# One store for an output that goes to four places, earlier query loads, and accumulations and weight loads spread out

## The chip, the cores and the metric

The kernel runs on one core of a Trainium2 chip. The time is what the device needs for one launch, in microseconds (us); three runs of the kernel before gave 1413.55, 1416.99 and 1418.76, median 1416.99. One further execution was taken with the hardware profiler; the page and the trace rows below are of that one. The engines are TensorE (PE in the rows; PEld is its weight load), VectorE (DVE), ScalarE (ACT), GpSimd (POOL) and SyncE (SP, whose DMA queue is SPq). They run their own instruction streams in order and wait for each other through semaphores.

## The reference

A pre-norm decoder layer in float32 on 2 batches of 512 rows of width 1024. The first block is causal attention with 32 query heads and 8 key/value heads of 128:

```python
q = (hidden_states @ Wq).reshape(B, S, nh, hd).transpose(0, 2, 1, 3)
k = (hidden_states @ Wk).reshape(B, S, nkv, hd).transpose(0, 2, 1, 3)
v = (hidden_states @ Wv).reshape(B, S, nkv, hd).transpose(0, 2, 1, 3)
q = _apply_rope(q, cos, sin)
k = _apply_rope(k, cos, sin)
logits = jnp.einsum('bhqd,bhkd->bhqk', q, k) * scale
attn = jax.nn.softmax(logits.astype(jnp.float32), axis=-1).astype(q.dtype)   # after the causal mask
out = jnp.einsum('bhqk,bhkd->bhqd', attn, v)
return out.transpose(0, 2, 1, 3).reshape(B, S, nh * hd) @ Wo
...
x = x + _L0_attn_ref(_layernorm(x, axis=-1), L0_attn_Wq, L0_attn_Wk, L0_attn_Wv, L0_attn_Wo)
x = x + _L0_xattn_ref(_layernorm(x, axis=-1), ctx_4096, ...)   # fake-quantised product, 1024x1024 per batch
x = x + _L0_ffn_ref(_layernorm(x, axis=-1), ...)               # low-rank experts, top 16 of 64
```

## The kernel before, in words

Every float32 product is made of three passes over a high and a low part (float32r), and the big products (queries, keys, values, output) use seven block products in place of eight. The seven are called P1 to P7.

From about 194 to 950 us of the span the program is a loop over 64 **units** `u`, one head of one batch each. `u // 8` is the key/value group, `u % 8 // 4` the batch. On TensorE a unit is: `scores(u)`, a place for work, `mix(u - 1)` (probabilities times values), a second place, `turn_probs(u)` (ten transposes of the probabilities); where a unit has a third place, it came between the second and `turn_probs(u)`. A **place** holds a **job**, one of the seven block products of a pair of query or key heads that a later unit will need. Units 3, 5, 8, 12 and 16 have three jobs, units 50 and 52 one, unit 56 none, the others two. From unit 57 on the places hold steps of the output projection (`first_step`).

For a job, ScalarE rounds a piece of the weight to its high part (`narrow_high`), GpSimd makes the low part (`narrow_low`), TensorE multiplies into one of two banks (`job_bank`, even and odd jobs), and VectorE reads the bank (`read_job`). So job j+2 waits until job j has been read. The results of jobs P4 and P3 are rotated: GpSimd ends the rotation (`turn_added`), and SyncE stores it to `qk_dram` (`keep_turned`), from where `load_q` fetches one head of one batch (256 KB) two units ahead. ScalarE needs that load in `q_high(u + 1)`, which stands right behind `probs_high(u - 1)` at the start of its unit u, ahead of the exponentials.

The output of a unit lies in bank 5 (`mixed`). ScalarE copies it to `o_st[u % 2]` (`keep_out`), and SyncE stores it. The output projection is also done with seven products, so it needs sums of quarters of the attention output: A00, A01, N11 (a negated A11), S1, S2, S3, S4. The stores put an output into every array of which it is the first summand: `O_STORES` names them, four arrays for the units 0 to 31 of batch 0 (16 units), one array for every other unit. The other summands are added in DRAM: GpSimd issues DMAs that accumulate 1 MB each (`accumulate`), three in a row at the end of its unit u when u % 8 is 2, and one when u % 8 is 6 from unit 32 on.

Then come 48 **steps** of the output projection (`step`, 24 matmuls each, from 950.5 us), six products of eight steps. A step needs 512 KB of `oraw` from DRAM (`load_step`) and a pair of rows of blocks of Wo, which lies in four buffers w00, w10, w11, w01 of eight pieces of 512 KB (`load_wo_early`: two pieces a unit from unit 53 on, 16 in all; the other 16 two a step in steps 2 to 9). After that the second and third blocks of the layer run, which the change does not touch.

The order on each engine is written out by hand in the loops over `u` (lines 605, 822, 1021, 1380 and 1617 in the profile's numbering).

## Time and profile before

| what | value |
|---|---|
| median of 3 runs | 1416.99 us |
| profiled execution | 1417.59 us |
| its span, first to last instruction | 1415.8 us |
| TensorE busy | 1297.9 us (92%) |
| VectorE, ScalarE, GpSimd busy | 830.5, 771.2, 611.3 us |
| mean granted TensorE clock | 0.966 of full |
| SyncE's DMA queue (q1) | 176.79 MB, 38.3% of the DMA engines' time |
| GpSimd's DMA queue (q0) | 29.36 MB, 10.5% |

TensorE is busy for 92% of the span. The page's idle column names for each group of instructions who released it; the forty slices show that TensorE's busy share falls below nine tenths at the start, in single slices of the unit loop, around 850 to 1000 us, and at the end.

### The profile page before, as it was taken

The page shows a single profiled execution, that of the slowest core. Times are in us where ns is not written, and L with a number is a line of the kernel's source. Part 1 is how long each engine was busy: PE and PEld are TensorE (multiplying, and loading weights), DVE is VectorE, ACT ScalarE, POOL GpSimd, SP SyncE. Part 2 cuts the span into 40 slices and gives each one's busy share as a digit, 9 for nine tenths or more (in the row PEclk, how much of TensorE's full clock was granted, in tenths as well). Part 3 has the DMA queues.
Part 4 walks back from the last instruction along what each step waited for, and adds up shares of the span by engine and source line. Part 5 has one row for each costly group of instructions (what it writes and reads, how often), then busy time and mean ns, then how long its engine had stood idle before and what let it go on. Part 6 is the DMA issues. An engine that isn't in the chain of part 4 may idle for free. (4 is left out here: it accounts for less than half of the span.)

```text
span 1415.8 us, 19913 instructions
## 1 busy us (share of the span) xinstructions
PE 1297.9 (92%) x7025; PEld 1111.4 (78%) x7025; DVE 830.5 (59%) x1805; ACT 771.2 (54%) x1587; POOL 611.3 (43%) x454
## 2 busy tenths in 40 slices
PE   4999998999799998999999978797999998987998
PEld 4879997778678887888888867685888887766777
DVE  7687134354455554555656555353786778787863
ACT  4412246565566775777777767672333355465440
POOL 5676656566477665777776644220000000021000
PEclk9899999999899999999999998898999999999999
DMA  7033144437638548467385756849643385200001
GB/s 252 8 127 120 62 146 159 122 102 181 205 97 206 196 141 254 142 152 196 104 223 146 185 159 214 241 132 290 250 137 117 123 270 188 91 1 16 31 30 45
DMA packets 117122, 207.42 MB, mean 147 GB/s; under 512 B 10128, under 2 KB 51088, under 8 KB 113440
## 3 DMA queue, kind: packets, MB, share of 16 engines
q1 hardware_dynamic: 112992, 176.79, 38.3%
q0 software_dynamic: 4032, 29.36, 10.5%
q8 instruction: 56, 0.92, 0.3%
q14 instruction: 42, 0.34, 0.1%
HBM read 147.40 MB, written 88.08 MB: 166 GB/s over the span
## 5 line engine op out<-in xcount | busy, mean ns | idle before, releaser
L1215 DVE TENSOR_TENSOR pT_lo<-banks,pT_hi 128x512 fp32r<-128x512 f32 (+1 forms) x192 | 104.0, 596 | 234.2 <-ACT pT_hi L953 234.0
L1790 POOL TENSOR_TENSOR resid<-resid,colterm 128x1024 f32<-128x1024 f32 x8 | 19.9, 2493 | 370.8 <-ACT colterm L1847 281.2
L1553 PE MATMUL banks<-xc,nring_hi_b 128*128 128x512 f32 x448 | 148.1, 413 | 20.0 <-DVE n_u L1165 8.0
L1595 PE MATMUL banks<-ob_hi,oa_hi 128*128 128x512 f32 x384 | 152.1, 396 | 12.7 <-DVE ob_lo L1247 12.7
L1595 PE MATMUL banks<-ob_lo,oa_hi 128*128 128x512 f32 x384 | 151.5, 394 | 0.0
L1595 PE MATMUL banks<-ob_hi,oa_lo 128*128 128x512 f32 x384 | 151.1, 393 | 0.0
L1553 PE MATMUL banks<-xc,nring_hi_a 128*128 128x512 f32 x448 | 140.9, 396 | 5.9 <-DVE q_made L1165 5.9
L953 ACT CAST pT_hi<-banks 128x512 fp32r<-128x512 f32 (+1 forms) x192 | 86.8, 523 | 107.3 <-PE banks L1523 107.1
L937 ACT CAST oa_hi<-oraw 128x1024 fp32r<-128x1024 f32 x48 | 50.4, 1049 | 159.6 <-PE banks L1595 136.5
L719 POOL TENSOR_TENSOR q_lo<-q_raw,q_hi 128x512 fp32r<-128x512 f32 x64 | 89.8, 1405 | 107.0 <-ACT q_hi L891 107.0
L1523 PE MATMUL banks<-ident,prob 128*128 128x128 f32 x640 | 85.5, 283 | 30.8 <-ACT o_st L979 29.7
L1553 PEld LDWEIGHTS banks<-xc,nring_hi_b 128*128 128x128 f32 x448 | 85.0, 199 | 36.5 <-issue 15.3
L1224 DVE CUSTOM_DVE_ANT_0 prob<-banks,mask 128x512 f32<-128x512 f32 (+3 forms) x256 | 110.1, 485 | 1.3 <-PE banks L1509 0.8
L1523 PEld LDWEIGHTS banks<-ident,prob 128*128 128x128 f32 x640 | 77.3, 147 | 41.3 <-issue 33.5
L1244 DVE TENSOR_TENSOR oa_lo<-oraw,oa_hi 128x1024 fp32r<-128x1024 f32 x48 | 58.8, 1224 | 76.5 <-ACT oa_hi L937 76.1
L1553 PEld LDWEIGHTS banks<-xc,nring_hi_a 128*128 128x128 f32 x448 | 80.7, 189 | 20.3 <-POOL nring_lo_b L724 3.6
L1595 PEld LDWEIGHTS banks<-ob_hi,oa_hi 128*128 128x128 f32 x384 | 73.3, 191 | 29.5 <-issue 14.3
L1553 PE MATMUL banks<-xc,nring_lo_b 128*128 128x512 f32 x224 | 91.3, 408 | 0.0
L1509 PE MATMUL banks<-kT_hi,q_hi 128*128 128x512 f32 (+3 forms) x256 | 89.2, 349 | 0.0
L1485 PE MATMUL banks<-xc,wring 128*128 128x512 f32 x336 | 83.9, 411 | 5.3 <-DVE banks L1140 3.3
L960 ACT ACTIVATE banks<-prob,small 128x384 f32<-128x384 f32 (+2 forms) x192 | 88.2, 459 | 0.7 <-DVE small L1224 0.7
L1553 PE MATMUL banks<-xc,nring_lo_a 128*128 128x512 f32 x224 | 88.1, 393 | 0.0
(245 smaller groups left out, 3480.0 us busy)
## 6 DMA issues: line engine op xcount, KB each, us to landing
q_raw<-qk_dram SPq DMA_DIRECT2D x64, 256.0 KB, 3.5
o_S<-o_st SPq DMA_DIRECT2D x64, 256.0 KB, 3.8
w<-in_L_attn_Wo SPq DMA_DIRECT2D x32, 512.0 KB, 6.4
oraw<-o_S SPq DMA_DIRECT2D x32, 512.0 KB, 3.6
nraw<-in_L_attn_Wq SPq DMA_DIRECT2D x28, 512.0 KB, 5.0
o_S<-o_S POOLq DMA_DIRECT2D x12, 1024.0 KB, 12.6
o_S<-o_N POOLq DMA_DIRECT2D x12, 1024.0 KB, 13.8
resid<-in_x SPq DMA_DIRECT2D x16, 512.0 KB, 5.2
```

What stands on the lines that cost most here:

```text
L719: nc.gpsimd.tensor_tensor(qh[1][:, u % 2, :], q_raw[:, u % 2, :], as32(qh[0][:, u % 2, :]), ALU.subtract).then_inc(q_lo, 1)
L937: nc.scalar.copy(oa[0][:, s % 2, :, :], oraw[:, s % 2, :, :]).then_inc(oa_hi, 1)
L953: nc.scalar.copy(pT[0][:, CHUNKS[c][0]:CHUNKS[c][0] + CHUNK_WIDTH[c]], turned_chunk(turned, mixed, c)).then_inc(pT_hi, 1)
L960: nc.scalar.activation(prob[:, sl] if n == 0 else score_tile(i), prob[:, sl], ACT.Exp, bias=shift[:, i:i + 1], scale=-1.0, accum_out=total ...
L1215: nc.vector.tensor_tensor(pT[1][:, sl], turned_chunk(turned, mixed, c), as32(pT[0][:, sl]), ALU.subtract).then_inc(pT_lo, 1)
L1224: nc.vector.tensor_tensor_reduce(out=prob[:, PROB_AT[i]:PROB_AT[i] + w], in0=score[:, s, c:c + w], in1=mask[:, H - w:H], scale=-SCALE, sca ...
L1244: nc.vector.tensor_tensor(oa[1][:, s % 2, :, :], oraw[:, s % 2, :, :], as32(oa[0][:, s % 2, :, :]), ALU.subtract).then_inc(oa_lo, 1)
L1485: ins = nc.tensor.matmul(dst, wring[:, a, n % 3, k * 256 + fb * P:k * 256 + (fb + 1) * P], xc[:, XI[p], c, k, :], start=first, stop=(k == ...
L1509: ins = nc.tensor.matmul(score[:, s, c:c + w], qh[a][:, u % 2, i * P:(i + 1) * P], kT[e][:, h % 2, 0:w], start=(p == 0), stop=(p == 2))
L1523: ins = nc.tensor.transpose(dst[:, col:col + P], prob[:, PROB_AT[i] + j * P:PROB_AT[i] + (j + 1) * P], ident[:])
L1553: ins = nc.tensor.matmul(job_bank(j), n_ring(a, j)[:, k * P:(k + 1) * P], xc[:, XI[p], c, k, :], start=(opens and k == 0 and n == 0), stop ...
L1595: ins = nc.tensor.matmul(step_bank(m, t), oa[a][:, s % 2, k, t * P:(t + 1) * P], ob[c][:, s % 2, k, :], start=(q == 0 and k == 0 and i == ...
```

## The change

Eight edits, all in the attention part:

1. The seven output arrays become slices of one DRAM tensor `o_all`, ordered so that A00, S2, S3, S4 lie side by side. SyncE's `keep_out` issues one DMA whose source is `o_st` broadcast over the names, in place of one DMA a name. The bytes written are the same.
2. SyncE issues `load_q(u + 2)` before `keep_turned` of the job at (u - 1, 0), except where that store is what the load reads (`tight`).
3. The accumulations of a group are issued one a unit, at the end of GpSimd's units u % 8 = 2, 3 and 4; those of the last group one after the units, one after 4 and one after 16 output steps. `load_step` waits for fewer of them at the first step of a product and for the rest at the seventh.
4. Wo: 20 pieces in place of 16 are loaded in the units, and the remaining 12 one a step in steps 2 to 13; w01 comes before w11.
5. ScalarE copies the output (`keep_out(u - 1)`) right behind `normalise_wide(u)`, ahead of `narrow_high` of later jobs, of `first_high` and of the copies of banks.
6. VectorE reads the second job of a unit with three jobs at the end of that unit; before, it did so in the next unit, behind `probs_low` and `peaks`.
7. TensorE does the transposes of a unit with three jobs before its third job.
8. Of the ten transposes only the last two, which go into bank 5, wait for the output's copy (`o_copied`).

```diff
-EARLY = 2 * PAIRS
+EARLY = 2 * PAIRS + PAIRS // 2
+WO_PIECES = [(n, q) for n in (0, 1, 3, 2) for q in range(PAIRS)]
+O_NAMES = ("A00", "S2", "S3", "S4", "S1", "A01", "N11")
...
+        o_all = nc.dram_tensor("o_all", [len(O_NAMES), 2 * PAIRS, P, H], F32, kind="Internal").ap()
...
     def o_count(u):
-        return 16 * sum(len(o_names(v)) for v in range(u % 2, u + 1, 2))
+        return 16 * len(range(u % 2, u + 1, 2))
...
         def keep_out(u):
             sp.wait_ge(o_copied, u + 1)
-            for name in o_names(u):
-                sp.dma_start(o_dram[name][o_place(u)[1]], o_st[u % 2][:]).then_inc(o_kept[u % 2], 16)
+            names = o_names(u)
+            n = O_NAMES.index(names[0])
+            sp.dma_start(o_dram["all"][n:n + len(names), o_place(u)[1]].rearrange("n p c -> p n c"),
+                         o_st[u % 2][:].unsqueeze(1).to_broadcast([P, len(names), H])).then_inc(o_kept[u % 2], 16)
...
             if q == 0 and name[0] == "S":
-                sp.wait_ge(s_added[name], 16 * {"S1": 4, "S2": 8, "S3": 4, "S4": 12}[name])
+                sp.wait_ge(s_added[name], 16 * {"S1": 3, "S2": 7, "S3": 4, "S4": 10}[name])
+            elif q == PAIRS - 2 and name in ("S1", "S2", "S4"):
+                sp.wait_ge(s_added[name], 16 * {"S1": 4, "S2": 8, "S4": 12}[name])
...
         for u in range(1, UNITS):
+            tight = u + 2 < UNITS and (u - 1, 0) in JOB_AT and JOB_AT[u - 1, 0] == turning_job(u + 2)
+            if u + 2 < UNITS and not tight:
+                load_q(u + 2)
             if (u - 1, 0) in JOB_AT:
                 keep_turned(JOB_AT[u - 1, 0])
-            if u + 2 < UNITS:
+            if tight:
                 load_q(u + 2)
...
-            if s < 2 + PAIRS:
-                load_wo_early(2 * PAIRS + s - 2)
-                load_wo_early(3 * PAIRS + s - 2)
+            if EARLY + s - 2 < len(WO_PIECES):
+                load_wo_early(EARLY + s - 2)
...
-            if u % 8 == 2 and u >= 8:
-                accumulate_negated(u // 8 - 1)
+            if 2 <= u % 8 <= 4 and u >= 8:
+                accumulate_negated(u // 8 - 1, u % 8 - 2)
...
-        accumulate_negated(GROUPS - 1)
+        accumulate_negated(GROUPS - 1, 0)
+        pool.wait_ge(step_done, 4)
+        accumulate_negated(GROUPS - 1, 1)
+        pool.wait_ge(step_done, 2 * PAIRS)
+        accumulate_negated(GROUPS - 1, 2)
...
             normalise_wide(u)
+            if u > 0:
+                keep_out(u - 1)
             for j in jobs_of(u + 1)[1:]:
                 narrow_high(j)
...
-            if u > 0:
-                keep_out(u - 1)
...
-            for p in (1, 2):
-                if (u - 1, p) in JOB_AT:
-                    read_job(JOB_AT[u - 1, p])
+            if (u - 1, 2) in JOB_AT:
+                read_job(JOB_AT[u - 1, 2])
+            elif (u - 1, 1) in JOB_AT:
+                read_job(JOB_AT[u - 1, 1])
...
             if (u, 0) in JOB_AT:
                 read_job(JOB_AT[u, 0])
+            if (u, 2) in JOB_AT:
+                read_job(JOB_AT[u, 1])
...
-                pe.wait_ge(o_copied, u)
             for c in range(3):
+                if c == 2 and u > 0:
+                    pe.wait_ge(o_copied, u)
...
             place(u, 1)
+            turn_probs(u)
             place(u, 2)
-            turn_probs(u)
```

How the order moves at three places. First VectorE behind unit 3, which has three jobs. Before, unit 4 begins (`pT_lo` and four row maxima, the last of which is the first row here), and only then stand the reads of the jobs (3, 1), four instructions that end in n_u, and (3, 2), three that end in q_made, and the two reciprocals of unit 4's row sums:

```order
L1224 ISA prob,small<-banks,mask 128x256
L1224 ISA small 128x1
L1185 TENSOR_TENSOR n_u<-banks,n_u 128x512
L1186 TENSOR_TENSOR banks<-banks,n_u 128x512
L1164 TENSOR_TENSOR n_sin<-banks,sin 128x512
L1165 TENSOR_TENSOR n_u<-banks,cos 128x512
L1194 TENSOR_TENSOR banks<-banks,n_p 128x512
L1164 TENSOR_TENSOR q_made<-banks,sin 128x512
L1165 TENSOR_TENSOR q_made<-banks,cos 128x512
L1231 RECIPROCAL small<-small 128x1
L1233 RECIPROCAL small<-small 128x3
```

In the changed kernel the read of job (3, 1) stands ahead of unit 4's low parts and maxima:

```order
L1199 TENSOR_TENSOR n_u<-banks,n_u 128x512
L1200 TENSOR_TENSOR banks<-banks,n_u 128x512
L1178 TENSOR_TENSOR n_sin<-banks,sin 128x512
L1179 TENSOR_TENSOR n_u<-banks,cos 128x512
L1229 TENSOR_TENSOR pT_lo<-banks,pT_hi 128x512 x2
L1229 TENSOR_TENSOR pT_lo<-banks,pT_hi 128x256
L1238 ISA prob,small<-banks,mask 128x512
L1238 ISA small 128x1
L1238 ISA prob,small<-banks,mask 128x384
```

Four instructions moved up by one unit's head. Second, SyncE's queue in its units 10 and 11: behind the weight loads (nraw) the stores of one rotated half (n_turn), those of the other (n_sin, n_u), then the load of unit 13's queries (q_raw) and the stores of unit 9's output to four arrays:

```order
L496 DMA nraw<-in_L_attn_Wq 128x4x256 x2
L508 DMA qk_dram<-n_turn 64x512
L509 DMA qk_dram<-n_turn 64x512
L508 DMA qk_dram<-n_turn 64x512
L509 DMA qk_dram<-n_turn 64x512
L508 DMA qk_dram<-n_sin 64x512
L509 DMA qk_dram<-n_u 64x512
L508 DMA qk_dram<-n_sin 64x512
L509 DMA qk_dram<-n_u 64x512
L488 DMA q_raw<-qk_dram 128x512
L514 DMA o_A<-o_st 128x512
L514 DMA o_S<-o_st 128x512 x3
```

The same stretch in the changed kernel:

```order
L503 DMA nraw<-in_L_attn_Wq 128x4x256 x2
L515 DMA qk_dram<-n_turn 64x512
L516 DMA qk_dram<-n_turn 64x512
L515 DMA qk_dram<-n_turn 64x512
L516 DMA qk_dram<-n_turn 64x512
L495 DMA q_raw<-qk_dram 128x512
L515 DMA qk_dram<-n_sin 64x512
L516 DMA qk_dram<-n_u 64x512
L515 DMA qk_dram<-n_sin 64x512
L516 DMA qk_dram<-n_u 64x512
L522 DMA o_all<-o_st 128x4x512
```

The load now stands ahead of the second set of stores, whose rotation it does not need, and the four output stores are one. Third, GpSimd from its unit 42 on: three accumulating DMAs stood together, ahead of the low part of the queries (q_lo) and of those of the job weights:

```order
L741 TENSOR_TENSOR nraw<-nraw 128x4x128
L765 DMA o_S<-o_N 128x2048 x3
L719 TENSOR_TENSOR q_lo<-q_raw,q_hi 128x512
L724 TENSOR_TENSOR nring_lo_b<-nraw,nring_hi_b 128x512 x2
L730 TENSOR_TENSOR nraw<-n_ta,nraw 128x4x2x64
L719 TENSOR_TENSOR q_lo<-q_raw,q_hi 128x512
```

In the changed kernel:

```order
L754 TENSOR_TENSOR nraw<-nraw 128x4x128
L778 DMA o_all<-o_all 128x2048
L732 TENSOR_TENSOR q_lo<-q_raw,q_hi 128x512
L737 TENSOR_TENSOR nring_lo_b<-nraw,nring_hi_b 128x512 x2
L743 TENSOR_TENSOR nraw<-n_ta,nraw 128x4x2x64
L778 DMA o_all<-o_all 128x2048
L732 TENSOR_TENSOR q_lo<-q_raw,q_hi 128x512
```

The second and third accumulation moved to the ends of the next two units.

## Rows read from the trace of the kernel before

**Rows 1.** Who TensorE waited for, whole span: total us, times, longest us.

```profile
PE banks L1523 <- ACT o_st L979: 29.7, 9, 11.4
```

**Rows 2.** TensorE by stretch: us, busy (instructions), granted clock, DMA share, GB/s.

```profile
293.40:306.60 13.20, 13.20 (x74) 1.00 0.69 181
659.90:670.30 10.40, 10.40 (x61) 1.00 0.69 157
...
992.40:1003.30 10.90, 10.90 (x49) 1.00 0.84 296
```

**Rows 3.** The same view, units 4 to 17 behind three jobs.

```profile
238.00:255.00 17.00, 12.98 (x62) 0.80 0.30 85
...
416.10:430.10 14.00, 10.58 (x60) 1.00 0.71 192
sum 78.20, PE 61.35; mean PE 12.27
```

**Rows 4.** The same view, units 12, 28 and 52.

```profile
343.50:366.00 22.50, 15.97 (x72) 0.85 1.00 293
539.80:555.50 15.70, 11.53 (x61) 0.92 1.03 320
793.40:804.40 11.00, 8.76 (x49) 0.89 1.03 206
```

**Rows 5.** The same view: units 27, 56 and 60; output steps 0 to 4.

```profile
525.10:539.80 14.70, 12.23 (x61) 0.88 0.80 163
837.20:854.80 17.60, 6.17 (x37) 0.76 0.67 176
889.00:908.90 19.90, 11.54 (x61) 0.80 1.02 287
...
950.50:992.40 41.90, 33.04 (x123) 0.84 0.95 282
```

**Rows 6.** VectorE, timeline: start, us, what, [idle before, releaser].

```profile
243.34 0.68 DVE L1165 TENSOR_TENSOR n_u<-banks,cos 128x512 f32<-128x512 f32 x1
...
532.20 0.70 DVE L1199 TENSOR_TENSOR banks<-banks,n_u 128x512 f32<-128x512 f32 x1 [3.56 <-POOL n_turn L759]
...
852.19 1.45 DVE L1238 TENSOR_TENSOR ob_lo<-w,ob_hi 128x1024 fp32r<-128x1024 f32 x1 [9.36 <-ACT ob_hi L922]
```

**Rows 7.** ScalarE, timeline, where it waited for a load.

```profile
355.24 0.62 ACT L891 CAST q_hi<-q_raw 128x512 fp32r<-128x512 f32 x1 [10.79 <-DMA q_raw<-qk_dram]
...
850.60 0.62 ACT L920 CAST oa_hi<-oraw 128x512 fp32r<-128x512 f32 x1 [5.99 <-DMA oraw<-o_A]
...
904.66 0.62 ACT L920 CAST oa_hi<-oraw 128x512 fp32r<-128x512 f32 x1 [8.38 <-DMA oraw<-o_A]
```

**Rows 8.** SyncE's queue, timeline: issues.

```profile
332.53 0.61 SPq L509 DMA_DIRECT2D qk_dram<-n_turn  x1
...
342.16 0.53 SPq L488 DMA_DIRECT2D q_raw<-qk_dram  x1
...
345.81 5.37 SPq L514 DMA_DIRECT2D o_S<-o_st  x3
...
847.76 1.07 SPq L543 DMA_DIRECT2D oraw<-o_A  x2
```

**Rows 9.** GpSimd, timeline: three accumulations issued in unit 10.

```profile
334.42 2.66 POOL L765 DMA_DIRECT2D o_S<-o_S  x3
```

**Rows 10.** The page's DMA queues: packets, MB, share of 16 engines.

```profile
q1 hardware_dynamic: 112992, 176.79, 38.3%
q0 software_dynamic: 4032, 29.36, 10.5%
```

**Rows 11.** DMA issues by line: count, KB each, median us to landing.

```profile
q_raw<-qk_dram SPq DMA_DIRECT2D x64, 256.0 KB, 3.5
o_S<-o_st SPq DMA_DIRECT2D x64, 256.0 KB, 3.8
w<-in_L_attn_Wo SPq DMA_DIRECT2D x32, 512.0 KB, 6.4
```

More of the change, by code:

```diff
@@ L129, in build @@
         v_dram = nc.dram_tensor("v_dram", [NB * S, GROUPS * HEAD], F32, kind="Internal").ap()
-        o_dram = {n: nc.dram_tensor(f"o_{n}", [2 * PAIRS, P, H], F32, kind="Internal").ap()
-                  for n in ("A00", "A01", "N11", "S1", "S2", "S3", "S4")}
+        o_all = nc.dram_tensor("o_all", [len(O_NAMES), 2 * PAIRS, P, H], F32, kind="Internal").ap()
+        o_dram = {name: o_all[n] for n, name in enumerate(O_NAMES)}
+        o_dram["all"] = o_all
         with ExitStack() as first:
@@ L522, in load_wo_early @@
         def load_wo_early(n):
-            which, q = n // PAIRS, n % PAIRS
-            if n % PAIRS == 0:
+            which, q = WO_PIECES[n]
+            if q == 0:
                 sp.wait_ge(job_done, JOBS - (4, 1, 3, 0)[which])
@@ L767, in accumulate, with accumulate_negated @@
                                 accum_op=ALU.add, max_dma_last_dim=8192).then_inc(s_added[name], 16)
[L769 to L771 removed]
+        def accumulate_negated(g, n):
+            if n == 0:
+                for v in (8 * g + 6, 8 * g + 7):
+                    pool.wait_ge(o_kept[v % 2], o_count(v))
             if g < 4:
[L773 to L779 removed]
+                accumulate(("S2", "S3", "S4")[n], "S1", g, g)
+            else:
+                accumulate(("S4", "S2", "S1")[n], "N11", g, (4 + 2 * (g - 4) + 1, g, g - 4)[n])
         def accumulate_plain(g):
```

11 lines of the change are left out of this document (2 added, 9 removed).

## The prediction

> **What bounds the kernel now.** I read the page first: TensorE is busy for 1297.9 of 1415.8 us, so the time is TensorE's work plus what it waits, plus what slow clock costs it. Then the waits of TensorE: in the unit loop the largest entry is the transposes waiting for ScalarE's copy of the output, 29.7 us in nine waits, one of 11.4 [rows 1]. Nine waits in 64 units are accidents of single units, not a rhythm. So I cut TensorE's time at the starts of the units. A clean unit with two jobs takes 10.4 us, one with three 13.2, both without a gap at full clock [rows 2]; so a job is worth 2.8, a one-job unit 7.6 and unit 56, with none, 4.8. A clean output step takes 10.9 / 2 = 5.45 [rows 2]. What a unit takes above that is its loss, idle time and half-clock time together: where TensorE had stood still, the granted clock of these stretches is 0.76 to 0.92 [rows 4, 5]. Last I looked up, on the other engines, what each loss was waiting for.
>
> **The sum, term by term** (losses that go are gains).
>
> *Behind the three-job units.* Units 4, 6, 9, 13 and 17 take 78.2 us together, 52.0 if clean: 26.2 lost [rows 3]. Job (4, 0) writes the bank of job (3, 1), whose read ended on VectorE at 243.34 + 0.68 = 244.0 [rows 6], behind unit 4's low parts and maxima, which need unit 4's scores. In the changed order that read stands at the end of unit 3, when its job has just ended, and TensorE has the third job (2.8) and the next scores ahead of the bank's next use. The read itself, 2.6 us for four instructions of 0.68, delays VectorE's low parts, but these are used only after scores and a job. The hardest case is unit 16, where the moved read waits for a rotation on GpSimd that begins after the read before it; I put that read's end about 1.5 us ahead of its need. The transposes move 2.8 earlier in these units; a two-job unit has them there already. Gain: 25 of 26.2 (bounds 18 and 26).
>
> *Query loads.* Units 12, 28 and 52 lose 22.5 − 13.2 = 9.3, 15.7 − 10.4 = 5.3 and 11.0 − 7.6 = 3.4, together 18.0 [rows 4]. In unit 12 ScalarE stood for 10.79 us for the queries of unit 13, which began to be rounded at 355.24 [rows 7]. The load had been issued at 342.16 [rows 8]: 13.1 us to land, where the median is 3.5 [rows 11]. Three accumulations of 1 MB had gone out at 334.42 [rows 9]. The change attacks both ends. The load stands ahead of stores that waited for a rotation; the stores before it had ended at 332.53 + 0.61 = 333.1 [rows 8], so it can go 9 us earlier, before any accumulation. And the queues hold less at once. SyncE's queue moves 176.79 MB in 38.3% of 1415.8 = 542 us of all 16 engines, 326 GB/s or 3.2 us for 1,048,576 bytes, and GpSimd's 28 accumulations take 10.5% = 149 us, 5.3 each [rows 10]. Three at once are 16 us of all engines; one a unit is 5.3 beside some 6 for the unit's other 2 MB (2 x 3.2), about 11.4 in 10.4 us: nearly full, for three units of eight. So I leave one microsecond: gain 17 (bounds 9 and 18).
>
> *Unit 27* loses 14.7 − 10.4 = 4.3 [rows 5]. VectorE waited 3.56 for a rotation [rows 6] behind three accumulation issues on GpSimd; such three took 2.66 us [rows 9], so one takes 0.9. The wait shrinks by 1.7, TensorE's idle time to under 1: gain 3.3 (bounds 1.5 and 4.3).
>
> *Unit 56* loses 17.6 − 4.8 = 12.8 [rows 5]. The transposes waited for the output's copy, which stood on ScalarE behind the rounding of the first piece of A00, and that waited 5.99 for its load until 850.60 [rows 7]. With the copy ahead the transposes go about 8 us sooner, but what is late next is the same load: issued at 847.76 [rows 8], it is behind stores that wait for the last rotation, and no edit moves it. The first step's weight low part ends at 852.19 + 1.45 = 853.6 [rows 6]; TensorE began that step some 4 us later, and will begin it there. The second step then waits 1.4 for VectorE. Gain: 2.7 (bounds 0 and 8).
>
> *Unit 60* loses 19.9 − 10.4 = 9.5 [rows 5]: ScalarE stood 8.38 for a load of A00 that landed behind three accumulations and 1 MB of Wo [rows 7]. With one accumulation a unit, the same arithmetic as above (here 2 MB of loads and stores beside it) leaves a latency near the 8 us that the double buffer hides. Gain: 7 (bounds 3 and 9.5).
>
> *Output steps 0 to 4* take 41.9, clean 27.3: 14.6 lost, at a DMA share of 0.95 [rows 5]. There the last three accumulations, 1 MB of Wo a step and 0.5 MB of `oraw` a step met. Now it is one accumulation, 0.5 MB of Wo a step, and the other two later. What is new is that the pieces of w11 come late: the fourth is issued behind the load of step 9 and is used by step 8. At 5.45 a step it goes out some 2.8 us after step 6 ends, and step 8 starts 8.1 later; rounding it (1.0) and its low part (1.2 to 1.45, [rows 6]) leave 5.8 us to land, where 6.4 is the median of a Wo piece [rows 11]: up to 0.6 lost. Steps 10 and 11 carry another 2 MB of x, which may cost the second half of w11 as much again. Gain: 13 (bounds 7 and 14.6).
>
> *The small ones.* Four of the nine waits for the copy are in the units above; of the other five, and of the slow clock behind the long ones, I take 3 us (bounds 0 and 6, a guess in the scale of [rows 1]). Edit 8, the later wait of the transposes, is worth at most the 0.8 us of eight transposes where the copy is just late; it is in these 3.
>
> *The single store.* Bytes are the same. Three DMA issues go in each of 16 units, 0.5 us each on SyncE, and once 5.37 us, when the queue was full [rows 8]; SyncE is not the bound, so I count it at nothing beyond the loads that go out sooner. If its cover is gone (a load right behind it), it is 1.5 us a unit in my favour.
>
> 25 + 17 + 3.3 + 2.7 + 7 + 13 + 3 = 71.0. The profiled execution took 1417.6 (span 1415.8), 0.6 above the median of the runs: 1417.6 − 71.0 = 1346.6, in the terms of the median 1346. I forecast 1346.6. By the optimistic ends 86.4 go, 1331; by the cautious ones 38.5, 1379.
>
> **Two rules of the skill against the rows.** The four stores landed in a median of 3.8 us each [rows 11], issued half a microsecond apart, so they overlap. The Trainium skill (DMA: Bandwidth & Descriptors, Anatomy of one DMA) gives each DMA a fixed part of about 2 us besides its bytes, and its section Bandwidth advises batches of 1 MiB and more. Read as time in the queue that would be an estimated 3 x 2 x 16 = 96 us of queue time saved; by the rows it is latency that overlaps, and the sum by them has nothing for it.
>
> The Wo loads, partitions outermost and two runs inside, land in 6.4 us for 512 KB [rows 11]; the new store has the same form with four runs. The Trainium skill (same page, Why a DMA increments its semaphore by 16) says that a DMA is spread over as many of the 16 engines as divide the slowest dimension as the instruction carries it. By this rule the new store, carried as 128x4x512, keeps all 16 and the sum stays; carried with the four copies outermost it would run on four. No row of the trace before shows a copy on four engines. The first rival below is that case.
>
> **Rivals.**
>
> *A, slower: the single store runs on a quarter of the engines.* Then its 1 MB takes 4 x 3.2 = 12.9 us where it now takes 3.2, and the query load queued behind it on these engines is 10 us late, as in unit 12. There such a lateness cost 9.3; in 16 units that is 149, and 1346.6 + 149 = 1496. It decides from 71 / 16 = 4.4 us a unit on. For it: queues are already at a share of 1.00 in such units [rows 4]. Against it: the form of the store, and loads that now go out 9 us sooner. Chance 0.04.
>
> *B: the transfers still collide.* The same bytes cross in the same eight units of each group, and one accumulation now falls into three units, all with four-fold stores, in place of one. If nothing of the DMA terms goes (17 + 7 + 13 = 37), the time is 1383.6; if half, 1365. For it: the 11.4 us of traffic in 10.4. Against it: the early load, and the clean units at a share of 0.69 [rows 2]. Chance 0.17, both together.
>
> *C: the stalls are passed on.* ScalarE's copy now stands ahead of roundings and waits for `mix`; VectorE reads more per three-job unit; a unit without its stall meets the next late thing at once. If each of the ten lossy units keeps 6 of its loss, 60 remain and the time is 1407 to 1410. Against it: the clean units have the same chain on ScalarE and VectorE and no gap [rows 2]. Chance 0.05.
>
> **Numbers.** Main case 0.74, with its own range 1334 to 1360. Faster and slower are measured from 1417.0; half a percent, 7 us, is about what a measurement of this kernel can tell from no change. Faster by more: main, B and nearly all of C, 0.93; within: 0.03; slower: A, 0.04. The range of 8 in 10 takes in the half of B: 1332 to 1376.
>
> **What would show it.** Right: units 4, 6, 9, 13 and 17 at 10.4 in the new trace; no wait of ScalarE for `q_raw` above 2 us; about 4.8 + 10 in unit 56, with TensorE waiting there for the first output step and not for the copy; output steps 0 to 4 under 29 us; the granted clock above 0.98. Wrong: `q_raw` landing in over 8 us behind `o_all` stores (A or B); new waits of TensorE on `nring` low parts or on ScalarE's `prob` (C); a wait of ScalarE or VectorE for `w` at steps 8 and 12 (the late w11).

## The result, and the profile after

The changed kernel takes 1347.25 us (median of 4 runs, 1344.87 to 1349.05) against 1416.24 for the kernel before on the same chip: ratio 0.9512, interval 0.9486 to 0.9538. The prediction was 1346.6. The profiled execution's span is 1343.9 us, 71.9 less than before. The page of the changed kernel, first the busy time of TensorE, then the clock that it was granted in forty slices, then the two DMA queues:

```profile
PE 1273.6 (95%) x7016; PEld 1094.8 (81%) x7025; DVE 832.2 (62%) x1805; ACT 773.2 (58%) x1587; POOL 612.5 (46%) x454
...
PEclk9999999999999999999999989999999999989999
...
q1 hardware_dynamic: 112224, 176.79, 40.4%
q0 software_dynamic: 4032, 29.36, 11.7%
```

TensorE is busy for 24 us less with the same work, because less of it runs at reduced clock (mean granted clock 0.987, before 0.966), and idle for 48 us less. The bytes are those of [rows 10].

The waits of TensorE, whole span (total us, times, longest us). The entry of [rows 1], nine waits for the output's copy, is gone from the list; these are the new or remaining ones of the unit loop and the output steps:

```profile
PE banks L1587 <- issue: 6.0, 1, 6.0
PE banks L1541 <- ACT prob L986: 5.9, 3, 3.3
PE banks L1613 <- DVE ob_lo L1261: 3.8, 2, 2.9
...
PE banks L1587 <- ACT p L942: 2.1, 1, 2.1
PE banks L1587 <- POOL oa_lo L798: 2.0, 1, 2.0
...
PE banks L1571 <- DVE q_made L1179: 1.3, 1, 1.3
```

TensorE by stretch: first units 4, 6, 9, 13 and 17 with their sum, against [rows 3]. They have no gap and the full clock, 1.00 (the 2.4 GHz level). Columns: us, busy (instructions), granted clock, DMA share, GB/s.

```profile
233.70:244.00 10.30, 10.30 (x58) 1.00 0.50 145
...
379.80:390.20 10.40, 10.40 (x60) 1.00 0.74 180
sum 51.60, PE 51.60; mean PE 10.32
```

Then, with all engines' busy time, units 12, 28 and 52 (against [rows 4]); units 27, 56, 57, 59, 60 and 61, and output steps 0 to 4 (against [rows 5]):

```profile
322.30:335.50 13.20, 13.20 (x74) 11.45 (x71) 8.93 (x22) 9.67 (x24) 11.71 (x11) 1.00 1.04 299
495.60:506.00 10.40, 10.40 (x61) 9.13 (x60) 5.33 (x16) 7.49 (x20) 6.04 (x6) 1.00 1.03 258
742.50:751.90 9.40, 7.83 (x50) 6.95 (x47) 5.39 (x16) 7.23 (x20) 9.19 (x9) 1.00 1.02 195
...
483.80:495.60 11.80, 10.54 (x60) 9.15 (x59) 5.39 (x16) 7.93 (x21) 11.59 (x10) 1.00 0.69 147
783.10:791.50 8.40, 5.12 (x35) 4.68 (x34) 5.30 (x16) 6.06 (x17) 4.07 (x4) 1.00 0.50 127
791.50:811.00 19.50, 13.47 (x62) 11.33 (x60) 7.56 (x16) 11.67 (x25) 5.92 (x5) 0.74 0.86 269
821.40:835.60 14.20, 12.23 (x60) 10.29 (x58) 8.29 (x16) 10.34 (x24) 8.66 (x8) 0.88 0.58 138
835.60:846.00 10.40, 10.40 (x61) 9.13 (x60) 5.38 (x15) 8.61 (x20) 4.66 (x4) 1.00 1.02 292
846.00:860.30 14.30, 12.20 (x62) 10.32 (x60) 7.03 (x16) 11.25 (x25) 4.70 (x5) 0.88 1.00 296
890.70:918.20 27.50, 27.50 (x121) 22.77 (x122) 14.08 (x12) 10.95 (x13) 1.63 (x2) 1.00 0.91 265
```

A reader should see two things. Units 12, 28 and 60 and the output steps are clean at a DMA share of 0.91 to 1.04, about the share at which they stalled before (0.95 to 1.03). And unit 56 is shorter, but what it no longer waits for is waited for in unit 57, which had lost only 0.9 before and loses 9.1 now.

Set against the terms of the forecast (loss = time above the clean 10.4, 13.2, 7.6 or 4.8):

| term | predicted gain | measured |
|---|---|---|
| units 4, 6, 9, 13, 17 | 25 | 78.2 − 51.6 = 26.6 |
| units 12, 28, 52 | 17 | 49.2 − 33.0 = 16.2 |
| unit 27 | 3.3 | 14.7 − 11.8 = 2.9 |
| unit 56 | 2.7 | 9.2 there, 8.2 lost again in unit 57: 1.0 |
| unit 60 | 7 | 9.5 there, 4.9 lost again in units 59 and 61: 4.6 |
| output steps 0 to 4 | 13 | 41.9 − 27.5 = 14.4 |
| small waits (19, 50, 53) | 3 | 4.1 |
| single store | 0 | see the fourth experiment |
| sum | 71.0 | 69.8 |

The span shrank by 71.9. The rest, some 2 us, is a balance of stretches outside the table. Unit 29 loses 0.4 less. The last unit's passage into the output steps takes 0.6 more. The first unit starts at 189.64 where it started at 194.02, in a stage whose code is the same and whose granted clock was 1.00 in one execution and 0.97 in the other; and behind output step 4 the changed kernel takes 2.3 us more (1343.9 − 918.2 against 1415.8 − 992.4). The first is no gain of an edit: in the traces of the eleven experiments, e11 with the changed kernel itself among them, the first unit starts between 191.3 and 192.9, and the third experiment's shows 0.97 in the first stage too. Nor is the second a loss: e2's trace, with the same code from there on, takes 423.5 us from output step 5 to its end (1343.8 − 920.3), as the kernel before does.

The same cuts in a second execution of the changed kernel (e11) give the same times within 0.1 for all units but three: 8.9 in unit 56 (8.4 here), 18.5 in unit 57 (19.5) and 13.3 in unit 61 (14.3). Differences of about 1 us in these three are no effect of an edit.

### The profile page after: what moved, and what is told of

Same layout as the page of the kernel before. It is cut to its first block and busy times, and to the rows that moved or that the text cites. A ratio compares the mean times of both kernels' runs of the same rounds, so it can differ in the third digit from the quotient of the medians.

```text
span 1343.9 us, 19861 instructions
## 1 busy us (share of the span) xinstructions
PE 1273.6 (95%) x7016; PEld 1094.8 (81%) x7025; DVE 832.2 (62%) x1805; ACT 773.2 (58%) x1587; POOL 612.5 (46%) x454
## 3 DMA queue, kind: packets, MB, share of 16 engines
q1 hardware_dynamic: 112224, 176.79, 40.4%
q0 software_dynamic: 4032, 29.36, 11.7%
## 5 line engine op out<-in xcount | busy, mean ns | idle before, releaser
L1571 PE MATMUL banks<-xc,nring_hi_b 128*128 128x512 f32 x448 | 140.1, 394 | 0.0
L732 POOL TENSOR_TENSOR q_lo<-q_raw,q_hi 128x512 fp32r<-128x512 f32 x64 | 87.0, 1360 | 38.0 <-ACT q_hi L905 37.9
L1571 PEld LDWEIGHTS banks<-xc,nring_hi_b 128*128 128x128 f32 x448 | 80.2, 188 | 14.0
L1571 PE MATMUL banks<-xc,nring_lo_b 128*128 128x512 f32 x224 | 87.7, 392 | 0.0
L737 POOL TENSOR_TENSOR nring_lo_a<-nraw,nring_hi_a 128x512 fp32r<-128x512 f32 x48 | 63.0, 1313 | 51.8 <-ACT nring_hi_a L919 51.8
L1541 PE MATMUL banks<-ident,prob 128*128 128x128 f32 x640 | 80.4, 273 | 5.9 <-ACT prob L986 5.9
L1613 PEld LDWEIGHTS banks<-ob_hi,oa_lo 128*128 128x128 f32 x384 | 72.5, 189 | 15.3
```

What stands on the lines that cost most here:

```text
L732: nc.gpsimd.tensor_tensor(qh[1][:, u % 2, :], q_raw[:, u % 2, :], as32(qh[0][:, u % 2, :]), ALU.subtract).then_inc(q_lo, 1)
L737: nc.gpsimd.tensor_tensor(split(n_ring(1, j)), n_factor(j), split(as32(n_ring(0, j))), ALU.subtract).then_inc(n_lo, 1)
L1541: ins = nc.tensor.transpose(dst[:, col:col + P], prob[:, PROB_AT[i] + j * P:PROB_AT[i] + (j + 1) * P], ident[:])
L1571: ins = nc.tensor.matmul(job_bank(j), n_ring(a, j)[:, k * P:(k + 1) * P], xc[:, XI[p], c, k, :], start=(opens and k == 0 and n == 0), stop ...
L1613: ins = nc.tensor.matmul(step_bank(m, t), oa[a][:, s % 2, k, t * P:(t + 1) * P], ob[c][:, s % 2, k, :], start=(q == 0 and k == 0 and i == ...
```

## The experiments

Each starts from the changed kernel and takes one part back, unless it says otherwise. All times are medians, ratios are to the kernel before on the same chip (1416.32, 1414.72 and 1415.44 us in the three groups of runs: the first four, the next four, the last three). A ratio is taken over all runs of a group and can differ by 0.001 from the quotient of two medians.

**e1: the reads of the jobs back in their old places (edits 6 and 7 undone).**

```diff
+            for p in (1, 2):
+                if (u - 1, p) in JOB_AT:
+                    read_job(JOB_AT[u - 1, p])
-            if (u - 1, 2) in JOB_AT:
-                read_job(JOB_AT[u - 1, 2])
-            elif (u - 1, 1) in JOB_AT:
-                read_job(JOB_AT[u - 1, 1])
...
-            if (u, 2) in JOB_AT:
-                read_job(JOB_AT[u, 1])
...
+            place(u, 2)
             turn_probs(u)
-            place(u, 2)
```

> The changed kernel (median 1347.2 us) with edits 6 and 7 undone: VectorE reads the second job of a three-job unit in the next unit again, and TensorE's transposes stand behind the third job again. Theory (each loss has its own cause, and this order is the cause of units 4, 6, 9, 13 and 17): those five units take 76 to 78 us together in place of 52, and the time is 1347 + 24 = 1371, between 1365 and 1374. Rival (the losses of the kernel before were passed from one to another, so one edit alone gives back only a part): under 10 us, 1357 at most, because the spread of accumulations and the early loads keep these units shorter too.

Measured: 1373.77 us, ratio 0.9704 (0.9685 to 0.9724), 26.5 above the changed kernel. Its trace, units 4 and 17 and the sum of the five, then the waits of TensorE that are new against the changed kernel:

```profile
235.70:251.90 16.20, 12.18 (x60) 10.28 (x59) 9.78 (x23) 8.07 (x21) 7.41 (x6) 0.89 0.42 120
...
401.40:418.20 16.80, 13.37 (x60) 11.17 (x59) 5.99 (x17) 8.10 (x21) 7.42 (x6) 0.80 0.61 172
sum 77.90, PE 61.03 PEld 51.63 DVE 41.13 ACT 39.88 POOL 31.91; mean PE 12.21 PEld 10.33 DVE 8.23 ACT 7.98 POOL 6.38
```

```profile
PE banks L1568 <- DVE n_u L1179: 8.1, 2, 4.0
...
PE banks L1568 <- DVE n_turn L1179: 5.4, 2, 2.7
...
PE banks L1568 <- DVE q_made L1179: 4.7, 2, 3.4
```

The sum of the five units is 77.9 again (before 78.2), and the wait is the predicted one: a job waiting for VectorE's read of the bank that it overwrites. TensorE waits 18.2 us in these rows, 1.25 of it in unit 27 as in the changed kernel; the other 9 of the 25.9 us that the five units lose is work at reduced clock, 0.80 to 0.89 in four of them. The term is shown for edits 6 and 7 together; no run takes back one of the two alone.

**e2: the query loads back behind the stores (edit 2 undone).**

```diff
-            tight = u + 2 < UNITS and (u - 1, 0) in JOB_AT and JOB_AT[u - 1, 0] == turning_job(u + 2)
-            if u + 2 < UNITS and not tight:
-                load_q(u + 2)
             if (u - 1, 0) in JOB_AT:
                 keep_turned(JOB_AT[u - 1, 0])
-            if tight:
+            if u + 2 < UNITS:
                 load_q(u + 2)
```

> The changed kernel with edit 2 undone: every query load stands behind the stores of the rotated halves again; one accumulation a unit stays. Theory (two causes together made the load late, its place in the queue and the three accumulations at once): with one accumulation a unit a load issued late lands in 4 to 8 us in place of 13, so units 12, 28 and 52 lose 1 to 3 us each, 1347 + 5 = 1352. Rival 1 (the place in the queue alone decides): all of the 18 us come back, 1364. Rival 2 (the accumulations alone decide): nothing comes back, 1347.

Measured: 1345.99 us, ratio 0.9508 (0.949 to 0.9527): no difference, so the second rival held and not the theory's 1352. Units 12 and 28 stay clean. The loads do come later, as ScalarE's waits for them show (in two traces of the changed kernel two waits with 2.2 us and three with 4.5):

```profile
ACT q_hi L902 <- DMA q_raw<-qk_dram: 8.9, 8, 2.1
```

Eight short waits, none above 2.1, are absorbed ahead of TensorE. The earlier place of the load is worth nothing here.

**e3: the three accumulations together again (edit 3 undone on GpSimd; `load_step` keeps its split waits), loads early.**

```diff
-            if 2 <= u % 8 <= 4 and u >= 8:
-                accumulate_negated(u // 8 - 1, u % 8 - 2)
+            if u % 8 == 2 and u >= 8:
+                for n in range(3):
+                    accumulate_negated(u // 8 - 1, n)
...
-        accumulate_negated(GROUPS - 1, 0)
-        pool.wait_ge(step_done, 4)
-        accumulate_negated(GROUPS - 1, 1)
-        pool.wait_ge(step_done, 2 * PAIRS)
-        accumulate_negated(GROUPS - 1, 2)
+        for n in range(3):
+            accumulate_negated(GROUPS - 1, n)
```

> The changed kernel with edit 3 undone on GpSimd: three accumulations of 1 MB stand together again, also the last three ahead of the output steps (the split waits of the step loads stay). Theory: the early loads keep the query loads whole, so units 12, 28 and 52 lose nothing or 1 us, but unit 27 loses its 4 again, unit 60 about 7 and output steps 0 to 4 about 6 (half of their 14.6, since the weight loads stay spread): 1347 + 16 = 1363. Rival (the queue's fullness decides whatever the order of the issues): the query loads come late too, another 12 to 18, 1375 to 1380. Other rival (the spread did nothing): 1347.

Measured: 1375.43 us, ratio 0.9714 (0.9693 to 0.9735), 28 above the changed kernel. Its trace by stretch, units 12 and 61:

```profile
324.60:346.70 22.10, 15.75 (x74) 13.19 (x73) 9.60 (x23) 9.50 (x24) 12.52 (x11) 0.85 1.03 303
860.40:882.30 21.90, 12.03 (x62) 10.24 (x59) 7.74 (x16) 12.72 (x27) 5.94 (x5) 0.77 0.71 238
```

Unit 12 takes 22.1 again (22.5 in [rows 4]), but not for the old reason. GpSimd, then SyncE's queue, then ScalarE, by the timeline of this kernel:

```profile
315.99 2.64 POOL L778 DMA_DIRECT2D o_all<-o_all  x3
```

```profile
323.64 0.59 SPq L522 DMA_DIRECT2D o_all<-o_st  x1
331.19 2.16 SPq L495 DMA_DIRECT2D q_raw<-qk_dram  x1
```

```profile
340.72 0.60 ACT L991 ACTIVATE o_st<-banks 128x512 f32<-128x512 f32 x1 [8.70 <-DMA o_all<-o_st]
...
342.94 0.65 ACT L903 CAST q_hi<-q_raw 128x512 fp32r<-128x512 f32 x1
```

ScalarE has no wait for the query load of unit 13 any more: before it reaches that rounding, its copy of unit 11's output stands 8.70 us for its buffer, of which there are two. The store of unit 9's output out of that buffer, 1 MB to four places, was issued at 323.64 and holds the copy until 340.72, 17.1 us later; the median of such stores is 6.7 in this trace too. The three accumulations had gone out 7.7 us ahead of it. So with the load out of the way the next transfer in line was late. Over the whole span:

```profile
ACT oa_hi L949 <- DMA oraw<-o_all: 21.4, 4, 11.5
...
ACT oa_hi L932 <- DMA oraw<-o_all: 14.4, 2, 8.9
ACT o_st L991 <- DMA o_all<-o_st: 13.8, 3, 8.7
...
ACT q_hi L903 <- DMA q_raw<-qk_dram: 0.2, 1, 0.2
```

The output loads (`oraw`) in unit 61 and in the output steps are hit in the same way; TensorE's longest wait in the steps is 7.6 us. By stretch, unit 12 takes 8.9 us more than in the changed kernel, units 27, 28, 52 and 53 together 5.7 more, unit 61 7.6 more, and output steps 0 to 4 take 9.8 more (37.1 for 27.3, from the first matmul of step 0 to that of step 5). The expectation of 1363 was missed: it had the early loads keep unit 12 whole. The first rival's time came, 1375, but not by its mechanism, since the query loads are not late.

**e4: four stores in place of one (edit 1 undone).**

```diff
-        return 16 * len(range(u % 2, u + 1, 2))
+        return 16 * sum(len(o_names(v)) for v in range(u % 2, u + 1, 2))
...
-            names = o_names(u)
-            n = O_NAMES.index(names[0])
-            sp.dma_start(o_dram["all"][n:n + len(names), o_place(u)[1]].rearrange("n p c -> p n c"),
-                         o_st[u % 2][:].unsqueeze(1).to_broadcast([P, len(names), H])).then_inc(o_kept[u % 2], 16)
+            for name in o_names(u):
+                sp.dma_start(o_dram[name][o_place(u)[1]], o_st[u % 2][:]).then_inc(o_kept[u % 2], 16)
```

> The changed kernel with edit 1 undone: one DMA for each of the four arrays again, in the 16 units that have four. Theory (the bytes are the same, SyncE is not the bound, the four overlap): 1347, within 1.5 us, and SyncE's issues are 48 more. Rival (the single store is what lets the queue keep up): the queue fills as it did before, where three issues took 5.37 us, loads come 2 to 5 us later in the units with four stores and an accumulation, and the time is 1355 or more. Opposite rival (one transfer of 1 MB holds the queue against the loads behind it): 1343 or less.

Measured: 1345.23 us, ratio 0.9504 (0.9484 to 0.9525), where the changed kernel has 0.9512: no difference that can be told. Its page's landing times, then those of the changed kernel (issues, KB each, median us to landing):

```profile
o_all<-o_st SPq DMA_DIRECT2D x112, 256.0 KB, 3.9
```

```profile
o_all<-o_st SPq DMA_DIRECT2D x16, 1024.0 KB, 6.7
...
o_all<-o_st SPq DMA_DIRECT2D x48, 256.0 KB, 3.5
```

The first row is of all 112 stores, the 64 of the sixteen units with four and the 48 single ones. The single store of 1 MB lands in 6.7 us, less than two of the 256 KB ones in a row, and far under the 12.9 us of transfer alone that the first rival gave a quarter of the engines.

**e5: the loads of Wo in their old order (edit 4 undone).**

```diff
-EARLY = 2 * PAIRS + PAIRS // 2
-WO_PIECES = [(n, q) for n in (0, 1, 3, 2) for q in range(PAIRS)]
+EARLY = 2 * PAIRS
+WO_PIECES = [(n, q) for n in (0, 1, 2, 3) for q in range(PAIRS)]
...
-            if EARLY + s - 2 < len(WO_PIECES):
-                load_wo_early(EARLY + s - 2)
+            if s < 2 + PAIRS:
+                load_wo_early(2 * PAIRS + s - 2)
+                load_wo_early(3 * PAIRS + s - 2)
```

> The changed kernel (1347.2 us) with edit 4 undone: 16 pieces of Wo in the units, the other 16 two a step in steps 2 to 9, w11 ahead of w01. Theory (after e3 the accumulations are known to fill the queues; the weight loads alone carry less than they can move): output steps 0 to 4 lose 2 to 6 us more than in the changed kernel, nothing changes in the units: 1347 + 4 = 1351. Rival (the weight loads were as much a cause there as the accumulations): 1355 or more, with ScalarE waiting over 8 us for oraw in the steps.

Measured: 1351.96 us, ratio 0.9567 (0.9549 to 0.9585): 4.7 to 6.2 above the two medians of the changed kernel, as expected (1351). The loss is in the first output steps, 33.5 us in place of 27.3 for steps 0 to 4, cut the same way, where a load of `oraw` behind two Wo pieces a step is late:

```profile
ACT oa_hi L952 <- DMA oraw<-o_all: 10.3, 2, 8.4
```

**e6: the copy of the output, and TensorE's wait for it, back (edits 5 and 8 undone).**

```diff
             normalise_wide(u)
-            if u > 0:
-                keep_out(u - 1)
...
                 keep_first(STEP_AT[u, 0])
+            if u > 0:
+                keep_out(u - 1)
...
+                pe.wait_ge(o_copied, u)
             for c in range(3):
-                if c == 2 and u > 0:
-                    pe.wait_ge(o_copied, u)
```

> The changed kernel with edits 5 and 8 undone: ScalarE copies the output last in its unit again, and all ten transposes wait for the copy. Theory: unit 56 and 57 lose 2.7 us more together, since what bounds them is the load of A00 and not the copy, and units 19, 50 and 61 1 to 2 us more: 1347 + 4 = 1351. Rival (the copy's place was the cause of unit 56's 11.4 us wait): 1355 or more. Opposite rival (the copy's place does nothing): 1347.

Measured: 1351.63 us, ratio 0.9554 (0.9534 to 0.9574), 4.4 to 5.8 above. TensorE's waits, and unit 56:

```profile
PE banks L1540 <- ACT o_st L993: 20.2, 8, 11.7
```

```profile
786.40:804.20 17.80, 6.07 (x36) 5.66 (x35) 6.92 (x18) 9.58 (x23) 6.83 (x6) 0.69 0.69 186
```

The wait of [rows 1] is back with 20.2 us in eight waits and costs only 5: 13.0 are lost in unit 56 instead of 3.6, but unit 57 then loses 1.2 instead of 9.1. The time was the expected one (1351), its places only in part: units 56 and 57 lose 1.5 more together (2.7 expected), units 50 and 52 1.6 more, unit 19 nothing, and unit 60, which was not named, 5.1 more, of which its neighbours 59 and 61 give back 3.9. This is the clearest lesson on summing waits from a profile in this study: 11.7 us of wait stood in front of a load that was late by nearly as much.

**e7: only the reads, the spread accumulations and the Wo order (edits 1, 2, 5 and 8 undone).** The edit is the sum of those of e2, e4 and e6.

> The changed kernel with edits 1, 2, 5 and 8 undone, so what is left of the change is the order of the reads and transposes (6, 7) and the spread of accumulations and weight loads (3, 4). Theory from e1 to e4 (these are all that moved the time): 1347 + 4 for the copy = 1351, so 65 of 69 us. Rival (the edits that gave nothing alone cover for each other: a late load is hidden only while the store in front of it is one transfer and the copy early): 1357 or more, with ScalarE waiting over 15 us in total for q_raw.

Measured: 1350.01 us, ratio 0.9554 (0.9526 to 0.9581), the same as e6. So edits 3, 4, 6 and 7 alone make some 64 of the 69 us (ratio 0.9554 against 0.9512), and the single store and the early load add nothing to each other either: ScalarE waits 5.1 us in total for `q_raw`, where the rival had over 15. The parts also add up: taken back one at a time, the reads (26.5), the accumulations (28), the Wo order and the copy (some 5 each) come to 64 to 70 us, by which of the two medians of the changed kernel one counts.

**e8: the seam of the two kinds of steps (changed kernel, four moves).** The loads of the first output step ahead of the stores of the last turned keys, the last job read at the end of its own unit, the low part of the first step ahead of those of keys and values, and the last first-step result stored ahead of the probabilities.

```diff
+            for f in steps_of(u + 1):
+                load_first(f)
...
+                if (u - 1, 1) in STEP_AT:
+                    keep_first(STEP_AT[u - 1, 1])
...
-            if (u, 2) in JOB_AT:
+            if (u, 2) in JOB_AT or u == LAST_JOB_UNIT:
```

> The changed kernel with four more moves, at the seam between jobs and output steps: SyncE issues the loads of A00 ahead of the stores of the last rotation, VectorE reads the last job at the end of unit 55, GpSimd makes the low part of the next A00 piece ahead of those of the keys, ScalarE copies the first half of the first product ahead of the transposed probabilities. Theory (units 56 and 57 lose 12.6 us because the load of A00 is issued behind stores it does not need; units 59 and 61 lose 3.8 and 3.9 for the order on GpSimd and ScalarE): the load goes out 5 to 8 us sooner, unit 57 loses 2 to 4 in place of 9.1, units 59 and 61 lose 1 each: 1347 - 12 = 1335. Rival (the load would meet a full queue or the first step waits for something else, the weight's low part): unit 57 keeps 7 or more, 1342 or more.

Measured: 1340.59 us, ratio 0.9488 (0.9467 to 0.9508): 5.2 and 6.7 below the two medians of the changed kernel. The intervals of the ratios overlap, so by itself this is a small gain and not a certain one; e9, which builds on it, is clear. What it waited for in unit 57 of the changed kernel, SyncE's queue first and then ScalarE:

```profile
792.88 0.60 SPq L516 DMA_DIRECT2D qk_dram<-n_u  x1
793.59 1.07 SPq L552 DMA_DIRECT2D oraw<-o_all  x2
```

```profile
796.60 0.62 ACT L934 CAST oa_hi<-oraw 128x512 fp32r<-128x512 f32 x1 [5.68 <-DMA oraw<-o_all]
```

With the load ahead of these stores units 56 and 57 lose 4.8 + 1.6 = 6.4 together, where they lost 12.7. The expected 1335 was missed in unit 61: it was to lose 1 and loses 8.4, more than in the changed kernel (3.9), behind an output load in e8's trace:

```profile
842.48 0.62 ACT L936 CAST oa_hi<-oraw 128x512 fp32r<-128x512 f32 x1 [5.05 <-DMA oraw<-o_all]
```

**e9: e8 with two accumulations out of the last units.** The second and third of group 6 go out behind output steps 4 and 18, those of group 7 behind 14 and 22.

```diff
-            if 2 <= u % 8 <= 4 and u >= 8:
+            if 2 <= u % 8 <= 4 and u >= 8 and (u < 58 or u % 8 == 2):
                 accumulate_negated(u // 8 - 1, u % 8 - 2)
...
+        accumulate_negated(GROUPS - 2, 1)
+        pool.wait_ge(step_done, 14)
         accumulate_negated(GROUPS - 1, 1)
-        pool.wait_ge(step_done, 2 * PAIRS)
+        pool.wait_ge(step_done, 18)
+        accumulate_negated(GROUPS - 2, 2)
+        pool.wait_ge(step_done, 22)
         accumulate_negated(GROUPS - 1, 2)
```

> e8 with two accumulations of the seventh group moved out of units 59 and 60 to behind output steps 4 and 18, the two of the last group behind steps 14 and 22. Theory (unit 61 loses 8.4 in e8 because the load of A00 lands late beside an accumulation and 1 MB of Wo a unit): units 60 and 61 lose 2 together, the output steps stay as they are, e8's 1340.6 - 6 = 1334. Rival (Wo and the unit's own transfers fill the queue by themselves): unit 61 keeps 6 or more, 1340. Opposite rival (the accumulation behind step 4 meets Wo, oraw and x): the output steps lose 4 or more, 1340 or more.

Measured: **1335.57 us** (1334.17 to 1337.81), ratio 0.9436 (0.942 to 0.9453), 10.2 below the changed kernel of the same group of runs (e11) and the fastest of the study; 1334 was expected. Its units 56, 57 and 61:

```profile
784.70:794.70 10.00, 6.57 (x37) 5.83 (x35) 5.41 (x16) 5.97 (x17) 4.36 (x4) 0.83 0.60 169
794.70:806.60 11.90, 10.83 (x60) 9.26 (x59) 6.14 (x16) 10.86 (x24) 5.58 (x4) 1.00 1.02 341
839.50:850.50 11.00, 10.79 (x60) 9.20 (x59) 5.89 (x16) 9.99 (x24) 4.41 (x4) 1.00 0.56 185
```

All units together lose 11.8 (23.5 in the changed kernel, 79.5 before). Output steps 0 to 4 take 27.3 as in the changed kernel, so the opposite rival did not come either.

**e10: e3 with a quarter of the bytes in each accumulation.** Each of the accumulations adds one block of the four; three quarters of the sums are left out, so its time stands for no complete kernel. It tells whether the issues and their place, or the bytes, make e3's stall.

```diff
-            nc.gpsimd.dma_start(out=o_dram[name][k:k + 4].rearrange("k p c -> (k p) c"),
-                                in_=o_dram[source][k:k + 4].rearrange("k p c -> (k p) c"),
+            nc.gpsimd.dma_start(out=o_dram[name][k:k + 1].rearrange("k p c -> (k p) c"),
+                                in_=o_dram[source][k:k + 1].rearrange("k p c -> (k p) c"),
```

> e3 (three accumulations together) with each accumulation over one block in place of four, 256 KB in place of 1 MB; three quarters of the sums are left out, so the output is not the reference's. It tells bytes from issues. Theory (the engines' time for three times 1 MB makes the load or the store late): the 28 us of e3 go, but for unit 27's 2 to 3 from GpSimd's three issues: 1348 to 1350, or a little less, since 21 MB less are moved. Rival (three issues in a row, not the bytes): 1370 or more, unit 12 loses 5 or more again.

Measured: 1346.87 us, ratio 0.9516 (0.95 to 0.9532): 28.6 below e3, as fast as the changed kernel, and a little below the expected 1348 to 1350. Units 12 and 61, and ScalarE's copy of the output in unit 12, without a wait:

```profile
324.00:337.20 13.20, 13.20 (x73) 11.45 (x71) 8.92 (x22) 9.37 (x24) 11.49 (x10) 1.00 0.93 322
851.00:862.60 11.60, 10.59 (x60) 9.11 (x59) 6.95 (x16) 10.40 (x24) 4.43 (x4) 1.00 0.49 160
```

```profile
331.19 0.59 ACT L991 ACTIVATE o_st<-banks 128x512 f32<-128x512 f32 x1
```

The issues stand together as in e3; three quarters of the bytes are gone (and two thirds of that queue's packets, 1344 for 4032), and the stall with them. Unit 27 still loses 4.6 here, as its wait is for GpSimd, which still issues three in a row.

**e11: the changed kernel once more**, beside e9 and e10.

> The changed kernel itself, on the same chip as e9: 1346 to 1348, ratio to the kernel before 0.951. It is run as the measure for e2 and e4, which came out 1 to 2 us below the changed kernel's first median: if it comes out at 1345 to 1347 here, those two edits are worth nothing that can be told.

Measured: 1345.81 us (1343.93 to 1350.22), ratio 0.9512 (0.949 to 0.9534). The two medians of the changed kernel are 1.4 apart, which is the scale below which nothing is claimed here.

## Why the prediction was right, point by point

*The jobs behind three.* Right in place, cause and size: 25 predicted, 26.6 in the trace, 26.5 by e1.

*Query loads.* The size was right (17 and 16.2), the cause only half; that the sum came out here is in part luck. The prediction said that the change "attacks both ends", the load's place in the queue and how much the queues hold at once, and it gave weight to the 9 us by which the load goes out earlier. e2 shows that the early place is worth nothing once the accumulations are spread, and e3 that it is worth nothing in unit 12 when they are not: the load arrives, and the output's copy waits 8.70 us for the store. What removed the stall in unit 12 is that at most one accumulation of 1 MB goes out in a unit, and e10 shows that the bytes, not the issues, are what counts. Unit 28 is another case: with the accumulations together it loses 1.5 in e3, where it lost 5.3 before, and with the spread but without edits 1, 2, 5 and 8 (e7) it is clean. There the other edits alone would have removed most of the loss too. The estimate of 11.4 us of traffic in a unit of 10.4 came near: the share is 1.03 in unit 28 and 1.04 in unit 12, and neither loses anything. The sign (no wait of ScalarE for `q_raw` above 2 us) held in one trace of the changed kernel, with 1.4, and just failed in the other, with 2.2.

*Unit 27.* Right: 2.9 of 3.3. VectorE's wait for the rotation is 2.35 where it was 3.56 [rows 6], and one accumulation stands ahead of it on GpSimd in place of three (0.81 us, where three took 2.66 in [rows 9]). The wait shrank by 1.2 and not by 1.7, and TensorE is still idle for 1.26, not for under 1.

*Unit 56.* The mechanism was right, the term too large (2.7, measured 1.0). The transposes went 8 us sooner and the next late thing was the same load of A00, as written. The prediction had the first step begin sooner by some 4 us, right behind VectorE's low part, and the second wait 1.4; in the trace TensorE stands 6.03 us ahead of the first step, and of the 9.1 that unit 57 loses the other 3 are its work at a granted clock of 0.74 (13.47 busy for 10.4). The prediction also looked at unit 56 alone, although the step stands in unit 57. Its sign "about 4.8 + 10 in unit 56" failed for that reason: it is 8.4 there and 19.5 in the next.

*Unit 60.* It is clean, but its neighbours 59 and 61 lose 3.8 and 3.9 where they lost 1.7 and 1.1. Net 4.6 for 7 predicted. The unit and its neighbours must be read together here. With the accumulations together (e3) unit 60 is clean as well and unit 61 takes 21.9; with the spread kept and the copy of the output late (e6) unit 60 takes 15.5. So what made unit 60 itself clean is the early copy, and what the spread does is to keep the load of A00 less late: the three units lose 12.3 before, 7.7 in the changed kernel, 13.7 in e3, 8.8 in e6. In e9, with two accumulations out of these units, unit 61 loses 0.6.

*Output steps.* 14.4 for 13. Both halves of the reason held: e5 shows 5 to 6 us for edit 4 (its fewer pieces a step and its order were not taken apart), and with the accumulations together (e3) TensorE waits up to 7.6 us in the steps. The late w11 exists (ScalarE waits 0.86 us for it at 931.05) and costs TensorE nothing.

*The single store.* Counted at nothing, and it is nothing (e4, e7). Of the fixed part of about 2 us that the Trainium skill (DMA: Bandwidth & Descriptors, Anatomy of one DMA) gives a DMA, the landing times show something like it, though the section is on DMAs that GpSimd issues and these are SyncE's: 6.7 us for 1 MB against 3.9 for 256 KB leaves an estimated 3 us that does not grow with the bytes. The four overlap, and the kernel's time shows nothing of it. The batches of 1 MiB and more that the Trainium skill advises (same page, Bandwidth) gained nothing here. The form with the copies outermost, which by the rule that the prediction cites would run on four engines, was not tried, so of the first rival only this is shown: the store as it is written doesn't do it.

*The rivals.* B, transfers that still collide, was refuted as a whole (1347 and not 1365 or more) but holds in small in units 59 and 61. C, stalls passed on, is what happened between units 56 and 57 and nowhere else of any size.

The errors, 1.7 too much in unit 56 and 2.4 too much in unit 60, and 1.2 in the queries and unit 27, stand against 1.6, 1.4 and 1.1 too little in the first term, the output steps and the small waits; that the total came out within a microsecond is in part luck, as is the 4.4 us by which the first stage ended sooner without an edit.

## What to carry to other kernels

When a load is late behind a burst of transfers, moving that load ahead can only choose another victim, as in unit 12 of e3; spread the burst, and test it by taking bytes away without moving an issue. Count a wait at the head of a queue only for what remains when the next late thing is subtracted, and cut the time at units and their neighbours together: what one unit gains may stand in the next. A read that frees a buffer belongs at the end of the stage that filled it, not at the start of the one that needs it: with the transposes moved along, that was 26.5 us here (e1), one of the two large terms beside the spread of the accumulations, 28 (e3).

## What the runs showed of the hardware that was not expected

Three accumulations from DRAM to DRAM, 3 MB, issued within 2.64 us on GpSimd's queue, held back a store of 1 MB that was issued 7.7 us behind them on SyncE's queue: it took 17.1 us, where such stores land in a median of 6.7 (e3). With a quarter of the bytes (e10) no copy waited for a store. From the accumulations' issue to the landing are 24.7 us. The engines' time for what was issued from then to 324.89, by the prediction's 5.3 us for an accumulation and 3.2 us a MB on SyncE's queue, is an estimated 3 x 5.3 + 2.75 x 3.2 = 24.7 (two stores, four pieces of rotated halves, one query load): it fits, though some later transfers shared the time. How the engines divide themselves between the two queues no run shows.

A store of 1 MB from one SBUF tile to four places in DRAM takes 6.7 us to land (median of 16); where four of 256 KB are issued together in its place, the median of all 256 KB stores is 3.9. The share of SyncE's queue over the span is 40.4% and 40.1%. Neither form moved the time of the kernel.

In the unit loop of the changed kernel the granted clock was below 1.00 only where TensorE had stood still: 0.74 in unit 57, with an idle stretch of 3.29 us just ahead of it and one of 6.03 in it, and 0.88 in units 59 and 61, with waits of 1.97 and 2.1. In e1 five waits of 2.7 to 4.0 us, 16.9 together, came with another 9 us of this kind, half as much again, in four of the five units. The same wait does not always cost the same: unit 59 waits 1.95 to 1.98 in eight of these traces and has a clock of 0.88 and 14.2 us in five of them (the changed kernel twice, e1, e5, e10) and 1.00 and 12.7 us in three (e2, e3, e4); and of the two waits of 2.69 us in e1, unit 6 has 0.88 and unit 9 has 1.00. What decides it no run shows, so some 2 us in a unit behind such a wait can come and go without an edit.
